# A gated state-space block repacked: four directions of 96 channels as three chunks of 128 rows, deltas and state sums as split products

## What is computed

```python
xn = ln(x, norm_w, norm_b)                       # over the 96 channels
p = xn @ w_in.T;  x1, x2 = p[..., :C], p[..., C:]
u = x1 @ ssm_in_w.T;  xss, z = silu(u[..., :C]), silu(u[..., C:])
xd = einsum('bhwd,kcd->bhwkc', xss, x_proj_w)    # per direction: rank 8, B 8, C 8
dt = softplus(einsum('bhwkr,kdr->bhwkd', dtr, dt_w) + dt_b)
bc = sum(Bv * Cv, axis=-1)
gain = sum(bc[..., None] * dt + Ds.reshape(K, C), axis=-2)
y = ln(xss * gain, out_norm_w, out_norm_b) * z
out = x + (y @ ssm_out_w.T) * silu(x2) @ w_out.T
```

## Times and profile before

| | |
|---|---|
| median of 3 runs | 5741.08 us (5737.75 to 5743.78) |
| profiled execution: span, first to last instruction | 5743.1 us |
| of it the first stage (to the end of its last write of X) | 702.8 us |
| busy over the whole span | PE 87%, DVE 81%, ACT 51%, POOL 67% |
| busy in 0 to 703 us | PE 615.2, DVE 484.6, ACT 471.8, POOL 0.2 us |

### The profile page before, as it was taken

The page is one execution under the profiler, slowest core; times in us unless marked ns, Lnnn a source line. Parts: engine busy times, 40 slices in busy tenths (PEclk is TensorE's granted clock), DMA queues, the critical chain, the costliest instruction groups (busy, mean ns, idle before and its releaser), DMA issues. The chain is left out here.

```text
span 5743.1 us, 74310 instructions
## 1 busy us (share of the span) xinstructions
PE 4971.3 (87%) x16018; PEld 2207.8 (38%) x16018; DVE 4640.4 (81%) x5047; ACT 2949.7 (51%) x4576; POOL 3832.2 (67%) x2568
## 2 busy tenths in 40 slices
PE   6999889897779999998297888888888888888887
PEld 1222256464256666665152222222222222222222
DVE  4876643434418989899797999999999999999996
ACT  5776544443311111111135777777777777777776
POOL 0000032322418898888786999989998999999993
PEclk9998899998889999998698999999999999999998
DMA  2000000001777787776405667667766666677663
GB/s 47 0 0 0 7 1 1 0 1 56 226 158 139 138 152 140 147 141 107 91 9 138 185 183 189 185 182 189 187 186 178 186 185 187 184 189 189 187 184 100
DMA packets 373418, 711.24 MB, mean 124 GB/s; under 512 B 76604, under 2 KB 111224, under 8 KB 358936
## 3 DMA queue, kind: packets, MB, share of 16 engines
q1 hardware_dynamic: 373144, 708.17, 50.2%
HBM read 575.33 MB, written 82.32 MB: 115 GB/s over the span
## 5 line engine op out<-in xcount | busy, mean ns | idle before, releaser
L2015 POOL TENSOR_TENSOR l_hc<-l_h,l_c_rep 128x512 f32<-128x512 f32 x1536 | 1929.8, 1276 | 216.0 <-DVE l_h L2069 187.1
L2069 DVE TENSOR_TENSOR_SCAN l_h<-l_p_da,l_h,l_bu 128x512 f32<-128x512 f32 x1120 | 1412.8, 1279 | 10.5 <-ACT l_p_da L1920 8.8
L1920 ACT ACTIVATE l_p_da<-l_p_da,l_a_neg 128x512 f32<-128x512 f32 x1536 | 1008.5, 658 | 733.8 <-PE l_p_da L1775 712.9
L1221 POOL TENSOR_TENSOR l2b_prod<-l2b_v,l2b_attn 128x1568 f32<-128x1568 f32 x276 | 937.3, 3461 | 242.9 <-DVE l2b_osum L1269 125.2
L1775 PE MATMUL l_p_da<-l_stacked,l_pick 96*128 96x512 f32 x1536 | 908.9, 593 | 191.3 <-DVE l_h L2069 179.1
L2054 DVE TENSOR_TENSOR l_bu<-l_du_rep,l_p_b 128x512 f32<-128x512 f32 x1280 | 855.7, 669 | 29.7 <-DMA l_du_rep<-du_scratch 22.5
L1775 PEld LDWEIGHTS l_p_da<-l_stacked,l_pick 96*128 96x128 f32 x1536 | 293.7, 192 | 1162.4 <-DVE l_h L2069 900.3
L1269 DVE TENSOR_REDUCE l2b_osum<-l2b_prod 128x32 f32<-128x1568 f32 x384 | 665.7, 1780 | 62.9 <-POOL l2b_prod L1221 59.2
L1783 PE MATMUL l_p_y<-l_hc,l_y_pick 128*32 128x512 f32 x3072 | 566.4, 626 | 74.3 <-POOL l_hc L2015 71.7
L1174 ACT ACTIVATE l2b_logits<-l2b_conv,l2b_this_b 98x512 f32<-98x512 f32 x96 | 66.2, 689 | 870.5 <-PE l2b_conv L1139 870.5
L615 POOL TENSOR_TENSOR l_w_pos_low<-l1a_w_sed,l_w_pos_high 96x1536 fp32r<-96x1536 f32 x1 | 4.1, 4123 | 711.2 <-DVE l_w_fc_high L595 711.2
(11 more groups left out here) (267 smaller groups left out, 8905.2 us busy)
## 6 DMA issues: line engine op xcount, KB each, us to landing
l_du_rep<-du_scratch SPq DMA_DIRECT2D x1536, 256.0 KB, 3.8
l2b_img_high<-qkv_scratch SPq DMA_DIRECT2D x192, 306.2 KB, 5.6
l2b_img_low<-qkv_scratch SPq DMA_DIRECT2D x192, 306.2 KB, 9.4
l_stacked<-l_parts SPq DMA_DIRECT2D x512, 96.0 KB, 2.7
l2b_v<-v_scratch SPq DMA_DIRECT2D x192, 152.0 KB, 6.4
qkv_scratch<-l2a_strip SPq DMA_DIRECT2D x32, 840.0 KB, 5.2
du_scratch<-l_du SPq DMA_DIRECT2D x128, 192.0 KB, 2.1
v_scratch<-l2a_v_strip SPq DMA_DIRECT2D x32, 228.0 KB, 4.2
```

What stands on the lines that cost most here:

```text
L1221: return eng.tensor_tensor(dst.rearrange("q x (dy dx) -> q x dy dx", dx=WIN), window, attn_half[:, :, unit % 2].rearrange("q x (dy dx) -> ...
L1920: act.activation(p_da[i % DAS][:], p_da[i % DAS][:], ACT.Exp, scale=a_neg[:, k * G + GRP[i]:k * G + GRP[i] + 1]).then_inc(s_da, 1)
L2015: pool.tensor_tensor(hc[:, (G * par + i) % HCS, :], h[:, i, :], c_rep[:, par, :], ALU.mult).then_inc(s_hc, 1)
L2069: dve.tensor_tensor_scan(h[:, i, way], p_da[i % DAS][:, way], of, state, ALU.mult, ALU.add).then_inc(s_h, 1)
```

## The change

Only `gated_ssm_block` and its table of weights change.

- **Packing.** The 4 x 96 = 384 rows of (direction, channel) are cut in 3 chunks of 128 rows. Deltas, softplus, and gains work on 3 tiles of 128 x 512, and no longer on 4 of 96 x 512. Abs stays per chunk, Exp and Ln run once over 128 x 1536.
- **Split products.** One float32 product `w_bcd` gives rank rows (twice), B rows and C rows (128 rows). The rank rows are split into a float32r part and its rest, stacked in 96 rows, and one float32r product per chunk gives the delta. The B*C product is split in the same way and meets `pick` in one float32r product per chunk.
- **Sum over directions** by TensorE: three accumulating float32 products with `fold`, read from PSUM by the one VectorE instruction that makes y.
- **Both norms in one.** The first norm of tile n and the second norm of tile n-8 share Square, Ln, Exp and the multiplication, 96 x 1024 at a time (`centered`, `variance`, `normalise`); the norm of x is now made 6 tiles ahead.
- **GpSimd** takes the scale and shift of both norms, the multiplication by z, and the addition of the two parts of softplus.
- **Projections and Silu in groups of four tiles**, ahead of every fourth step, so that ScalarE changes its tables twice per four tiles.
- **Four semaphores for the four input transfers**; the tile waits only for its own quarter. The steps are all written out (t = -2 to 34), without a hardware loop. Four tiles are normed one after the other ahead of the first step.

```diff
-            pe.wait_ge(s_x, 16 * B)
-            all_tiles(pe, step)
+            def centered(n):
+                if n >= GROUP and n % GROUP == 0 and n <= TILES:
+                    pe.wait_ge(s_silu, n - 1)
+                elif n:
+                    pe.wait_ge(s_nrm, n)
+                if n >= SLOTS:
+                    pe.wait_ge(s_y, n - SLOTS + 1)
+                    mm = pe.matmul(p_c[:, 0, :], center[:], a[:, n % SLOTS, :], start=True, stop=True)
+                if n < TILES:
+                    pe.wait_ge(s_x[n // (TILES // B)], 16)
+                    mm = pe.matmul(p_c[:, 1, :], center[:], X[:, tile(n)], start=True, stop=True)
+                mm.then_inc(s_c, 1)
...
+            def dt_mm(m, k):
+                if k == 0:
+                    pe.wait_ge(s_lo, m + 1)
+                    if m >= 2:
+                        pe.wait_ge(s_y, m - 1)
...
+                pe.matmul(p_chunk[k], w_dt[:, k, :], split[:, m % 2, :], start=True, stop=True).then_inc(s_dtm, 1)
+
+            def bc_mm(m, k):
...
+                if m + 1 < TILES:
+                    pe.wait_ge(s_abs, CHUNKS * (m + 1) + k + 1)
...
+                pe.matmul(p_chunk[k], pick[:, k, :], bc_split[:, m % 2, :], start=True, stop=True).then_inc(s_bcm, 1)
+
+            def sum_mm(m):
+                for k in range(CHUNKS):
+                    pe.wait_ge(s_gain, CHUNKS * m + k + 1)
+                    mm = pe.matmul(p_sum, fold[:, k, :], gain[:, k, :], start=k == 0, stop=k == CHUNKS - 1)
+                mm.then_inc(s_sum, 1)
+
+            def s_mm(m):
+                pe.wait_ge(s_yz, m + 1)
+                if m < TILES - 1:
+                    pe.wait_ge(s_ln, m + 10)
...
+            def dt_abs(m, k):
+                act.wait_ge(s_relu, CHUNKS * m + k + 1)
+                if m:
+                    act.wait_ge(s_dt, CHUNKS * (m - 1) + k + 1)
+                act.activation(log_part[:, k, :], p_chunk[k], ACT.Abs, bias=dt_bias[:, k:k + 1]).then_inc(s_abs, 1)
...
+        @block.gpsimd
+        def _(pool):
+            def affine_x(n):
+                pool.wait_ge(s_nrm, n + 1)
+                pool.tensor_scalar(a[:, n % SLOTS, :], nrm[:, 1, :], cols[:, 0:1], cols[:, 1:2],
+                                   ALU.mult, ALU.add).then_inc(s_xn, 1)
...
+            def add_log(m, k):
+                pool.wait_ge(s_log, m + 1)
+                of = dt[:, m % 2, k, :]
+                pool.tensor_tensor(of, of, log_part[:, k, :], ALU.add).then_inc(s_dt, 1)
```

More of the change, by code:

```diff
@@ new lines, in variance @@
+            def variance(n):
+                if n >= GROUP and n % GROUP == 0 and n <= TILES:
+                    pe.wait_ge(s_silu, n)
+                if n > SLOTS + 1:
+                    pe.wait_ge(s_sgd, n - SLOTS - 1)
+                    pe.wait_ge(s_out, n - SLOTS - 1)
+                pe.wait_ge(s_sq, n + 1)
+                for part in range(*parts_of(n).indices(2)):
+                    mm = pe.matmul(p_v[:, part, :], mean_w[:], sq[:, part, :], start=True, stop=True)
+                mm.then_inc(s_v, 1)
@@ new lines, in step @@
+            def step(t, of_t, of_next, of_second, norms, gated):
+                if norms:
+                    centered(t + 6)
+                if of_next:
+                    for k in range(CHUNKS):
+                        dt_mm(t + 1, k)
+                if of_second:
+                    bcd(t + 2)
+                if norms:
+                    variance(t + 6)
+                if of_t:
+                    for k in range(CHUNKS):
+                        bc_mm(t, k)
+                if gated:
+                    s_mm(t - 3)
+                if of_t:
+                    sum_mm(t)
+                if gated:
+                    o_mm(t - 3)
@@ L224, in _ @@
+            for n in range(GROUP):
+                centered(n)
+                variance(n)
+            all_steps(step, project)
         @block.scalar
         def _(act):
[L226 to L237 removed]
@@ new lines, in y_of, with step @@
+            def y_of(m):
+                dve.wait_ge(s_sum, m + 1)
+                dve.scalar_tensor_tensor(a[:, m % SLOTS, :], p_sum, d_sum[:], a[:, m % SLOTS, :],
+                                         ALU.add, ALU.mult).then_inc(s_y, 1)
+            def step(t, of_t, of_next, of_second, norms, gated):
+                if of_next:
+                    for k in range(CHUNKS):
+                        relu(t + 1, k)
+                    bc_high(t + 1)
+                if of_t:
+                    for k in range(CHUNKS):
+                        gains(t, k)
+                if gated:
+                    gate(t - 3)
+                if of_next:
+                    bc_low(t + 1)
+                if norms:
+                    normalise(t + 6)
+                if of_second:
+                    rank_low(t + 2)
+                if of_t:
+                    y_of(t)
+                if of_second:
+                    bc_product(t + 2)
+                if gated:
+                    write_x(t - 3)
```

522 lines of the change are left out of this document (250 added, 272 removed).

## The result

The changed kernel takes **5587.39 us** (median of 4 runs, 5583.01 to 5593.15); the kernel before, run beside it, 5741.75 (4 runs, 5737.75 to 5743.78). The ratio is 0.9726, 95% interval 0.9712 to 0.9740: faster by 2.7%, 154 us. The profiled execution took 5583.01 us, with a span of 5581.2, so 1.8 us lie around the span.

The account below looks back on a forecast made before the run. Bound: the first stage's TensorE instruction stream. Stage: 62 + 48 + 290.9 + 52.5 + 77 + 33 = 563 us, plus 26 for the clock, 589 against 702.8; kernel 5627 us, range 5588 to 5680.

Parts of the forecast that it names:

- Start and tiles ahead: Stage start: first tile at 18 us, four tiles normed in 28 us, 12 projections 16 us, step -2 at 62 us.
- Steps -2 to 1 with their group: First steps, not yet full: 6 + 8.5 + 11 + 11 us, and a group of 12 projections at 11.0 us.
- GpSimd's loop: Step limit: Abs of chunk 2 waits for GpSimd's log addition of the tile before; 12.8 us per step with hand-overs.
- x: Time of one scale-and-shift on GpSimd, between 0.54 and 1.28 us, taken as 1.0.
- Eight stand behind a wait: 8 x 1.02: TensorE's step: eight of ten float32 products cost 1.02 us behind a wait, two 0.86, together 9.9 us.
- I add the 5.5% of before: Clock allowance: the earlier kernel's half-clock loss of 5.5% on 468 us of steps and projections, 26 us.
- Last steps and drain: Stage end: steps 26 to 30, with no input tile to norm, 5 x 10.5 = 52.5 us; drain 33 us.
- the norm ahead is cheap and the clock holds: Rival, chance 0.15: GpSimd scale-and-shift 0.54 us, no half clock after the start, projections at 10 us: 5585 us.
- VectorE and GpSimd in each other's way: Rival, chance 0.2: cast, subtraction and GpSimd's work slow each other on the shared SBUF port; loop 14.2 us, kernel 5657 us.
- The packed step is bound by latency: Rival, chance 0.06: a 6.5 us dependent chain met twice per step makes steps of 15 us; kernel 5710 us.
- The clock stays low: Rival, chance 0.06: first stage's TensorE stream at half clock, kernel slower; 5800 us with 16 of 32 tiles so.

Follow-up runs that it names:

- experiment 1: Changed kernel with two buffers for the log part, so Abs waits for GpSimd's additions of two tiles back: 5545.99 us, ratio 0.9644.
- experiment 2: Changed kernel with the third log addition ahead of the multiplication by z on GpSimd: 5549.88 us, ratio 0.9655.
- experiment 8: Kernel before with its state sums padded by zeros from 32 to 96 rows: 5697.72 us, ratio 0.9918.
- experiment 5: Changed kernel with plain float32 products on 32 rows in place of the split ones: 5793.36 us, ratio 1.0072.
- experiment 7: Changed kernel with plain float32 products in place of the split ones, but on 96 rows: 5633.26 us, ratio 0.9809.
- experiment 10: Changed kernel with GpSimd's work moved to VectorE, the three log additions at the head of the next step: 5651.45 us, ratio 0.9827.
- experiment 4: Kernel before with its hardware loop written out, nothing else changed: 5797.19 us, ratio 1.0084.
- experiment 6: Kernel of experiment 1 with the state sums on 64 of their 96 rows: 5542.15 us, ratio 0.9641.

## Why the prediction came out as it did

The direction was right, and so was the place of the limit; the saving was 40 us too small. Two terms of the sum failed, the clock allowance of 26 us and the price of a float32 product behind a wait. By the steps of the forecast:

- **Start and tiles ahead: right.** 16.93 us against 18; 28.0 against 28; projections 12.6 against 16; step -2 at 57.6 against 62. Together 4.4 us.
- **Steps -2 to 1 with their group: right.** 47.8 us; by the forecast's terms 47.5.
- **GpSimd's loop: right as the limit, and nearly in size.** By the starts of GpSimd's multiplication (L448) the steps inside a group are 12.2 to 13.4 us apart, most of the longer ones with a fall of the clock; without one they are 12.43 on TensorE (L214), against 12.8. With x = 0.77 for the 1.0 that I took the forecast gives 12.8 - 0.46 = 12.3. Experiments 1 and 2 show its cause.
- **"Eight stand behind a wait: 8 x 1.02": wrong.** A wait that is already met costs nothing: the float32 products are 0.86 us apart. The 1.03 was 0.07 for a real pause and 0.10 for the 32-row product (experiment 8). A step of TensorE with its one short wait is 10.84 us, not 12.1, and a group of projections 12 x 0.86 = 10.3, not 11.0. From step 2 to step 26 the forecast has 368.4 us at full clock; measured are 359.9 with falls of the clock in them, and by the steps without a fall it would be about 351.
- **"I add the 5.5% of before": wrong, and the largest term.** The 26 us were counted as if the loss belonged to the chip. Experiments 5 and 7 show that float32 products on 32 rows can bring it, and in experiment 8 it is gone from the kernel before once they are padded (with a shorter step besides); the change removes them. Something is lost all the same, 0.95 in 105 to 465 us, some 9 us, and experiment 1 shows with what: where the GpSimd stall is gone, so is the loss.
- **Last steps and drain: 2 us too short.** From step 26 to the end it took 87.6 us; forecast 85.5.

In sum: stage 589 forecast, 552.8 measured; of the 36 us, 4 lie ahead of step -2, 29 between steps 2 and 26 (20 of them the clock allowance on that stretch, 18 the over-priced products and x, less 9 for the falls that did come), the other 3 are the allowance of the other steps, less the drain. A further 4 us of the 154 come from outside the stage, by runs of the same instructions.

One reading of rows was loose and did no harm: 512 columns more cost ScalarE 0.47 us by the two rows named (1.06 - 0.59), not 0.43; the Square of 1024 columns took 1.02 and the Ln of 1536 took 1.48, as forecast.

Of the rivals, *the norm ahead is cheap and the clock holds* (0.15) gave 5585 us and was nearly met in number, but in part by luck: x is 0.77, between its 0.54 and my 1.0, the clock still falls, and the over-priced products, which it left as they were, made up for both. *VectorE and GpSimd in each other's way* is half there: the cast takes 0.40 us with GpSimd silent (experiment 10) and 0.78 at 240.84 beside the multiplication, 0.69 in the mean, and GpSimd's addition that starts beside it takes 1.45 us where two others take 2.51 together. But the cast has room on VectorE. The subtraction (L385) takes 0.68 us with and without GpSimd's work in the stage; at 247.44 GpSimd is idle beside it. By the Trainium skill ("GPSIMD Engine Reference", "1. Specifications") this contention was to be expected; the trace agrees for the cast, and experiment 1 shows that it doesn't set the step: the cast is as long there (0.77 us in most steps), and the steps take 10.79. *The packed step is bound by latency* did not happen: it had steps of 15 us, and experiment 1 has 10.79. *The clock stays low* did not happen to the changed kernel, but it did to experiment 5, which is slower than before with 0.80. The Trainium skill ("TensorE: Matmul & The Clock Gate", "HAM oscillation — how this bites in real kernels") lays half clock on idle gaps. Experiment 1 against the changed kernel fits that in kind, and so does experiment 10; experiment 5, with TensorE busy 535.00 of 535 us, does not, nor does experiment 8, which keeps its pauses of 0.8 to 0.9 us at a clock of 0.99.

How much each part brought, as the experiments price it: split products in place of 32-row float32 199 us, of which 151 is only the 32 rows; GpSimd's help 58, falls of the clock included; the early start 19. They overlap and do not add to 154, since the change also adds work (the sum over directions, one deep start).

What stays open: by what rule the clock falls. It moved with the rows of the products (experiments 5 and 7), with the pauses for GpSimd (experiment 1), and between experiment 4 and the kernel before with hardly more than the period of the steps. No run here separates how, nor whether rows act by themselves or by the late weight loads.

## What to carry to other kernels

A float32 product over 32 rows that stands among products over 96 can be padded with zero rows: it cost no time here and brought 47 us to a kernel that was otherwise unchanged. Before a longer spacing is charged to a wait, look whether its neighbours have the same shape, and whether the weight load starts ahead of its product. And before a run without a gain is taken to clear a cause, look whether a wait beside it has shrunk (experiment 6). After work is moved to a slower engine, look for the buffer that it holds: a second buffer, or its release ahead of an unrelated instruction, brought 47 and 41 us. And a loss of clock belongs to a pattern of work; it isn't carried over as a percentage.

## What the runs showed of the hardware

- Float32 products of 512 columns follow each other by 0.86 us at full clock for 96 and 128 rows, with met waits or without (experiment 7), and by 0.90 to 0.93 behind a real pause (L214 in the changed kernel, L186 in experiment 8).
- Between products over 96 rows the weight load started 0.43 us ahead of its product. Where the rows changed from 96 to 32 or back it started with the product, and the spacing was 0.95 to 1.03 us (kernel before and experiment 5); a float32r product over 64 rows behind a float32 one over 96 had the same late load (experiment 6).
- TensorE busy 535.00 of 535 us had a granted clock of 0.80 with six float32 products of 32 rows per step, and busy 414.83 of 415 us 1.00 with the same ones on 96 rows. With float32r on 32 rows it had 1.00.
- Of steps of 18.58 us every third had a fall to half clock in it (experiment 4), of steps of 18.67 to 18.76 with the same products 3 of 30.
- At the start of the changed kernel the record of the granted clock shows 1.00 while products last 2.02 us, twice as long as later.
- GpSimd: scale and shift of 96 x 512 float32 0.77 us; addition of 128 x 512 1.30 us.
